# A four-layer graph network on one core: counts' logarithms added by GpSimd, heads' weighted sums taken by nodes

## The reference, cut to what matters

```
def gat_layer(x, W, a_src, a_dst, bias, src, dst, heads, out_c, concat):
    h = (x @ W).reshape(n, heads, out_c)
    al_s = jnp.einsum('nhc,hc->nh', h, a_src)
    al_d = jnp.einsum('nhc,hc->nh', h, a_dst)
    e = jax.nn.leaky_relu(al_s[src] + al_d[dst], NEG_SLOPE)
    m = jax.ops.segment_max(e, dst, num_segments=n)
    ex = jnp.exp(e - m[dst])
    z = jax.ops.segment_sum(ex, dst, num_segments=n)
    alpha = ex / (z[dst] + 1e-16)
    msg = h[src] * alpha[:, :, None]
    out = jax.ops.segment_sum(msg, dst, num_segments=n)
```

## Time and profile before

| | us |
|---|---|
| median of the three runs | 2178.45 |
| the profiled execution | 2181.19 |
| its span, first to last instruction | 2179.4 |
| TensorE busy | 1939.9 (89%) |
| VectorE busy | 1211.6 (56%) |
| ScalarE busy | 838.8 (38%) |
| GpSimd busy | 559.0 (26%) |

### The profile page before, as it was taken

The page is one execution under the profiler, slowest core; times in us unless marked ns, Lnnn a source line. Parts: engine busy times, 40 slices in busy tenths (PEclk is TensorE's granted clock), DMA queues, the critical chain, the costliest instruction groups (busy, mean ns, idle before and its releaser), DMA issues.

```text
span 2179.4 us, 34673 instructions
## 1 busy us (share of the span) xinstructions
PE 1939.9 (89%) x11166; PEld 1699.0 (78%) x11167; DVE 1211.6 (56%) x2275; ACT 838.8 (38%) x1125; POOL 559.0 (26%) x538
## 2 busy tenths in 40 slices
PE   5998998989999999779999999996788869878898
PEld 5887986759999977579999999996446857675676
DVE  7842223454443645565555655554555687756696
ACT  2221222332222223224555555553333128631676
POOL 0003765630000056434333444100772000000000
PEclk9999999999999999989999999998899989989999
DMA  5445667754556567657788887875883012100211
GB/s 163 151 154 167 178 170 259 267 163 127 168 168 196 172 232 246 197 175 236 263 274 267 276 265 253 285 236 184 266 271 126 8 37 61 66 15 8 68 61 54
DMA packets 203766, 377.74 MB, mean 173 GB/s; under 512 B 18937, under 2 KB 174378, under 8 KB 203670
## 3 DMA queue, kind: packets, MB, share of 16 engines
q1 hardware_dynamic: 171014, 245.57, 34.9%
q0 software_dynamic: 31216, 128.89, 18.7%
q10 hardware_dynamic: 1440, 1.97, 0.2%
HBM read 288.03 MB, written 88.33 MB: 173 GB/s over the span
## 4 chain that ended last, share of the span: by engine, by line
PE 38%; DVE 6%; issue 5%; DMA 4%; ACT 3%; another core or an unknown queue 1%; POOL 1%; ACTq 0%; SPq 0%; DVEq 0%; POOLq 0%
PE ps L1867 20%; PE ps L2084 4%; PE ps L2049 3%; DMA arena<-in_L_gnn_W_rel 3%; PE ps L1749 2%; PE ps L1896 2%; PE ps L2126 1%; PE ps L1744 1%; PE ps L2010 1%; PE ps L1669 1%; DMA arena<-U,ix 1%; DVE arena L1471 1%; POOL arena L529 1%; PE ps L2036 1%
## 5 line engine op out<-in xcount | busy, mean ns | idle before, releaser
L1867 PE MATMUL ps<-w_hi,hT_hi 128*128 128x384 f32 x2052 | 719.5, 351 | 45.8 <-ACT arena L615 13.8
L1867 PE MATMUL ps<-w_hi,hT_lo 128*128 128x384 f32 x2052 | 695.0, 339 | 0.3 <-issue 0.3
L1867 PE MATMUL ps<-w_lo,hT_hi 128*128 128x384 f32 x2052 | 694.9, 339 | 0.0
L1867 PEld LDWEIGHTS ps<-w_hi,hT_hi 128*128 128x128 f32 x2052 | 391.8, 191 | 55.8 <-issue 19.3
L1867 PEld LDWEIGHTS ps<-w_lo,hT_hi 128*128 128x128 f32 x2052 | 391.5, 191 | 0.4 <-issue 0.2
L529 POOL DMA_INDIRECT arena<-U,ix x252 | 272.1, 1080 | 465.4 <-DMA U<-arena 348.6
L1867 PEld LDWEIGHTS ps<-w_hi,hT_lo 128*128 128x128 f32 x2052 | 391.3, 191 | 0.0
L615 ACT ACTIVATE arena<-ps 128x384 f32<-128x384 f32 x160 | 78.2, 492 | 448.4 <-PE ps L1867 386.4
L1749 PE MATMUL ps<-arena,onehot 128*128 128x512 f32 x504 | 197.6, 516 | 20.1 <-DVE onehot_r L1087 7.5
L1749 PEld LDWEIGHTS ps<-arena,onehot 128*128 128x128 f32 x504 | 91.0, 199 | 99.9 <-issue 95.8
L565 POOL DMA_INDIRECT h<-h_d,lidx x68 | 91.5, 1346 | 295.6 <-PE ps L1896 252.0
(11 more groups left out here) (289 smaller groups left out, 2920.6 us busy)
## 6 DMA issues: line engine op xcount, KB each, us to landing
arena<-in_L_gnn_W_rel SPq DMA_DIRECT2D x74, 1152.0 KB, 6.2
U<-arena SPq DMA_DIRECT2D x292, 192.0 KB
arena<-in_L_gnn_W SPq DMA_DIRECT2D x36, 1152.0 KB
U<-z SPq DMA_DIRECT2D x28, 864.0 KB
arena<-rows_d SPq DMA_DIRECT2D x40, 320.0 KB, 3.4
arena<-in_L_gnn_root SPq DMA_DIRECT2D x4, 1152.0 KB
arena<-U,ix POOLq DMA_INDIRECT x252
arena<-in_L_gnn_W_root SPq DMA_DIRECT2D x2, 1152.0 KB
```

What stands on the lines that cost most here:

```text
L1867: ins = pe.matmul(acc, l, r[:, j, kt, :], start=(n == 0), stop=(n == 3 * KT - 1))
```

## The change

Three things change in the attention passes.

1. **The counts' logarithms.** PE no longer adds them. `zt[t]` gets CT added in place by GpSimd, one add of 128x640 fp32 a tile, between ACT's `z` and DVE's `logits` (`log_counts`). PE's `log_terms` shrinks to `row_terms`: two products of 320 columns a head in place of thirty. `logs` (ACT and DVE), `cl_hi`, `cl_lo` and `ident_r` go.
2. **The weighted sums.** The exponentials are the stationary operand now, five blocks of 128x128 a tile, and the head's 65 or 97 feature columns move. The sums come out by nodes and collect in one bank, `2 + head % 2`, which one product with zeros clears at a head's start.
3. **The way back.** `sums_copy` on ACT and `turned` on PE go. DVE's `head_out` reads the bank itself and waits for the head's last product.

```diff
+            def log_counts(n, it, m):
+
+                for i in range(m):
+                    t = i % NG
+                    pool.wait_ge(A[n]["z_ok"], 2 * NG * it + i + 1)
+                    pool.tensor_tensor(zt[:, t, :], zt[:, t, :], CT[:, t, :], ALU.add).then_inc(A[n]["g_ok"], 1)
+            pool.wait_ge(S["ct_ln"], 1)
...
-                def sums_copy(hd):
-
-                    c = HEADS[n][1]
-                    act.wait_ge(s["o_mm"], 5 * hd + 7)
-                    act.wait_ge(s["o_tp"], hd + 1)
-                    act.activation(oT[0:c + 1, :].rearrange("p (b n) -> p b n", b=2), ps[0:c + 1, 2:4, 0:NP // 2], cp).then_inc(s["o_cp"], 1)
...
-                dve.wait_ge(s["z_ok"], k + 1)
-                dve.wait_ge(s["c_ok"], k + 1)
+                dve.wait_ge(s["g_ok"], k + 1)
+                if t == 0:
+                    dve.wait_ge(s["c_ok"], 2 * it + i // NG + 1)
                 z = zt[:, t, :].rearrange("p (b n) -> p b n", b=2)
-                dve.tensor_tensor(z, z, terms(i % 2), ALU.add).then_inc(s["l_ok"], 1)
+                dve.tensor_tensor(z, z, terms(i // NG), ALU.add).then_inc(s["l_ok"], 1)
...
-                o = ps[:, 6, 0:NG * (c + 1)].rearrange("p (g c) -> p g c", c=c + 1)
-                dve.wait_ge(s["o_tp"], hd + 2)
+                o = ps[:, 2 + j, 0:NG * (c + 1)].rearrange("p (g c) -> p g c", c=c + 1)
+                dve.wait_ge(s["o_mm"], NG * hd + NG + 2)
...
-                for m, (l, r) in enumerate(((ident_r, cl_hi[:, t]), (ident_r, cl_lo[:, t]), (ones_r, mrow[:, j]))):
-                    for b in range(2):
-                        ins = pe.matmul(terms(i % 2)[:, b, :], l[:], r[:, NP // 2 * b:NP // 2 * (b + 1)], start=(m == 0), stop=(m == 2), skip_group_check=True)
...
+                pe.wait_ge(s["row_cp"], 2 * hd + 3)
+                if hd >= 2:
+                    pe.wait_ge(s["l_ok"], NG * (hd - 1))
+                for b in range(2):
+                    ins = pe.matmul(terms(hd % 2)[:, b, :], ones_r[:], mrow[:, hd % 2, CW * b:CW * (b + 1)], start=True, stop=True)
                 ins.then_inc(s["c_ok"], 1)
...
                         pe.wait_ge(s["p_ok"], k + 11)
-                        for b in range(2):
-                            ins = pe.matmul(ps[0:c + 1, 2 + b, 0:NP // 2], R[:, t, (c + 1) * hd:(c + 1) * (hd + 1)],
-                                            pt[:, k % 2, NP // 2 * b:NP // 2 * (b + 1)], start=(t == 0), stop=(t == NG - 1), skip_group_check=True)
+                        for g in range(NG):
+                            ins = pe.matmul(ps[:, 2 + hd % 2, (c + 1) * g:(c + 1) * (g + 1)], pt[:, k % 2, P * g:P * (g + 1)],
+                                            R[:, t, (c + 1) * hd:(c + 1) * (hd + 1)], start=False, stop=(t == NG - 1), skip_group_check=True)
                         ins.then_inc(s["o_mm"], 1)
```

More of the change, by code:

```diff
@@ L107, in parts_of @@
             return (late_hi, late_lo) if ph == 2 else (msg[:, 0], msg[:, 1])
-        cl_hi, cl_lo = (t[:].rearrange("p j k n -> p (j k n)")[:, 0:NG * NP].rearrange("p (g n) -> p g n", g=NG) for t in (w_hi, w_lo))
         counts = sb("counts", [P, 2, NG, NP])
@@ L597, in _ @@
             gathers(2)
+            def log_counts(n, it, m):
[4 more added lines that the diff above has]
+            pool.wait_ge(S["ct_ln"], 1)
+            for n in range(3):
+                if n == 1:
+                    log_counts(n, 0, NG)
+                else:
+                    with pool.Fori(0, HEADS[n][0] // 2) as it:
+                        log_counts(n, it, 2 * NG)
         @block.scalar
@@ L799, in _ @@
             dense(Q_G1, lambda g, k: R[:, g, 0:H2 * (C2 + 1)].rearrange("p (h c) -> p h c", c=C2 + 1)[:, 4 * k:4 * k + 4, 0:C2])
-            def logs(n, ts=range(NG)):
-                for t in ts:
-                    act.activation(cl_hi[:, t, :], CT[:, t, :], cp).then_inc(S["cl_hi"], 1)
             def rows(n):
@@ L1446, in scores @@
                 link(ins)
-            def logs(n, ts=range(NG)):
-                for t in ts:
-                    dve.wait_ge(S["cl_hi"], NG * n + t + 1)
-                    ins = dve.tensor_tensor(cl_lo[:, t, :], CT[:, t, :], cl_hi[:, t, :].bitcast(F32), ALU.subtract)
-                if NG - 1 in ts:
-                    ins.then_inc(A[n]["cl_ok"], 1)
             def maximum(n, it, j, groups):
@@ L2115, in _ @@
                 head_rows(1, 0, part)
-            first_terms(1)
-            for i in range(2, NG):
-                log_terms(1, 0, i)
+            row_terms(1, 0)
             pe.wait_ge(A[1]["p_ok"], NG + 10)
```

61 lines of the change are left out of this document (15 added, 46 removed).

## The result

The changed kernel takes 2238.82 us in the median of four runs (2236.35 to 2242.18), the kernel before 2177.81 on the same chip: a ratio of 1.0281, 95% interval 1.0258 to 1.0303. The change makes it 2.8% slower; the forecast was 2232.7 us, 2.5% slower. The profiled execution's span is 2238.0 us, 58.6 more than before.

What follows compares the result with a forecast made beforehand. PE was taken to bound the kernel, DVE close behind. Terms +18.7 (n = 0), +43 (n = 2), -8, -2 and +2.5 give +54.2 on the profiled 2181.19 us: 2235.4, less 2.7 for the median, 2232.7; range 2157 to 2262.

Steps and rivals of the forecast that it cites:

- The bound and its order: Attention passes before the change: PE sets the pace, 10.93 us a head in n = 0, 10.95 in n = 2; DVE close behind.
- the idle time I took off: Middle heads of n = 2: some 0.3 us of DVE idle time in 10.95, so its own work about 10.6 us.
- The first rival: Attention passes: no conflict between adds and DVE, 9.4 us a head in n = 0, 10.6 in n = 2; 2158 us, chance 0.24.
- TensorE after: Products by nodes: ten load-and-product pairs a tile at 0.115 us, 1.15 us a tile, some 7 us a head.
- the sign of this step being wrong: Profile after: the step on PE is wrong if DVE or ACT still wait for L2048, the products by nodes.
- The add: GpSimd's add per tile: 1.3 us, between 0.63 and 1.9; 6.5 us of a head, not binding by its own work.
- The conflict: Adds on GpSimd block DVE operations with two SBUF operands: 0.56 to 1.3 us an add, 0.93 taken, 4.65 a head.
- For n = 1 +2.5: Pass n = 1: add chain 0, but products of L2126 run about 5 us of work at half speed, +2.5 us.
- The last two heads and the ends: n = 0 and n = 2: -2 us for each of four last heads, -1 for each of two pass ends.
- ACT binds now: Last two heads of each pass: ACT's two activations a tile of at most 0.82 bind, 8.2 us a head for PE's 10.06.
- The clock: PE after the change, busy some 7 us in 10 to 15: a lasting fall to 1.2 GHz held for unlikely.
- the second rival: PE stays at 1.2 GHz: 13.4 us a head, 2230 us without a conflict, chance 0.10; with a conflict hidden behind DVE.

Runs made afterwards that it cites:

- experiment 1: The kernel before with the new products by nodes and `head_out`, but its own `log_terms` on TensorE and nothing on GpSimd: 2153.40 us, ratio 0.9957.
- experiment 4: The changed kernel with the maximum's second operand from a PSUM bank instead of mask `C`, from the third head of n = 0 and n = 2: 2191.39 us, ratio 1.0127.
- experiment 11: The kernel of experiment 1 with GpSimd adding the logarithms in the last two heads of n = 0 alone: 2150.76 us, ratio 0.9937.
- experiment 7: The changed kernel with GpSimd's add replaced by a minimum with a constant, one SBUF operand, counts' logarithms left out: 2207.81 us, ratio 1.0064.
- experiment 3: The changed kernel with DVE making the add itself, in place before `logits`, and nothing on GpSimd: 2221.40 us, ratio 1.0256.
- experiment 2: The changed kernel with the turned products, the copy and the transposes of the kernel before, GpSimd's adds kept: 2219.02 us, ratio 1.0243.
- experiment 5: The changed kernel with ten further products of 184 columns a tile on TensorE in n = 2, result unused: 2269.69 us, ratio 1.0329.

## Why the prediction was right, point by point

**The bound and its order: right, with one term off.** That TensorE set the pace before and that its relief would be worth little holds. But in n = 2 DVE was level with it: its own work is 10.94 us a head (experiment 1), not 10.6. The step that failed there is the idle time I took off; waits of 0.15 us on its own results belong to DVE's work. So no relief of TensorE could have gained in the middle heads of n = 2. The first rival's -3.5 us for them was never to be had.

**TensorE after: right at full clock only.** Ten products take 1.22 to 1.36 us a tile there, for the 1.15 taken, and 2.2 at half. In the middle heads nothing waits long for them, but in the last heads of n = 2 DVE and ACT do, by the prediction's own words the sign of this step being wrong.

**The add: 1.5 us, not 1.3.** Five in a row take 7.54 us in n = 1, where DVE waits for them; the prediction's other figure, 1.4, is nearer; in the mean of all it is 1774 ns, since GpSimd is held up too. That is within the limits of 1 and 1.9 us that the prediction set.

**The conflict: right in kind and place, and in size in part by luck.** The maximum lasts 1.4 to 2.15 us beside adds, `logits` keeps 0.82. The blocking of DVE as the second to come, which no run of before showed, is in the rows of experiments 4 and 11. Experiment 4 shows that it takes two SBUF operands on DVE. What the Trainium skill says (SBUF — State Buffer, "Who interferes with whom") agrees as far as the add goes. For GpSimd's operation with one SBUF operand the page would have the lock too, and for the whole instruction; experiment 7 shows DVE held up only for about the first 0.6 us of 1.9, and the measurement decides. Predicted were 14.05 and 15.25 us a head, measured 14.13 and 14.80: a price of 0.90 us in n = 0, against an own work of 9.6 and not 9.4 (experiment 3), and of 0.77 in n = 2, against 10.94 and not 10.6, for the 0.93 taken. In both, own work too small and price too large partly cancel. The price itself came near by luck: with the measured 1.5 us for an add its bounds would have been 0.77 and 1.51 and its middle 1.14, and the same sum about 2249 us. The measured prices lie in the lower part of these bounds because of where the adds fall, which no row of before could tell.

**The terms of the sum.** Predicted +18.7 for n = 0 and +43 for n = 2; measured 10.0 + 12.6 = +22.6 and 10.5 + 30.4 = +40.9. For n = 1 +2.5, measured +2.8 with all around it: its first products ran at 1.2 GHz for about 6 us. The last two heads and the ends were to give -10. n = 0 gave -6.8, n = 2 **+2.0**. The step that failed is the bound of n = 2's last heads: "ACT binds now" holds only at full clock. At 1.2 GHz TensorE binds with 10.38 and 10.83 us, and from the last exponential (2227.81 us) to `head_out` it took 4.20 us for 3.53, where I had forecast one less. The -3.0 ahead of the passes had no term. The sum was +54.2, the measurement is +58.6. They came so near in part because errors cancel: n = 0 cost 3.9 us more than forecast and the ends 5.2 more, n = 2's middle 2.1 less and the time ahead 3.0 less.

**The clock: the mechanism was dismissed wrongly.** "I hold a lasting fall for unlikely, as a slower PE is a busier one" is refuted: 0.50 through all of n = 2, with TensorE busy 18 us of 20. That it cost only the end is due to the conflict, which hides it, as the second rival said. Without the conflict it would decide: experiment 7's 12.22 us a head are TensorE's. The two effects don't add up but take turns, so removing one alone gains less than its share.

**The first rival,** no conflict and faster, is excluded by the result and by experiments 2, 4 and 5; the range's lower part rested on it.
